# Two graph layers on one core: the lifting of the near-ones moved from ScalarE to TensorE, and DVE's additions set behind the next quotient

## The reference

```python
edge_index = jnp.stack([src, dst])
h = jnp.maximum(_layernorm(x), 0.0)
# layer 0: per edge and channel a softmax over the edges of one target
msg = h[src] + edge_attr;  s = msg * beta
e = exp(s - segment_max(s, dst)[dst]);  denom = segment_sum(e, dst)
agg = segment_sum(msg * e / denom[dst], dst)
x = x + (agg @ H + bias) + h            # H: 128x128, made of phm_rule and W
h = jnp.maximum(_layernorm(x), 0.0)
# layer 1: attention with 4 heads, 32 channels each
x = x + elu(segment_sum(alpha * (h @ W.T)[src], dst))
```

## Time and profile before

| | us |
|---|---|
| time, median of 3 runs | 2254.29 (2253.85 to 2254.93) |
| the profiled execution's own time | 2258.94 |
| its span in the profile | 2257.2 |
| layer 0's sweep, about | 60 to 1086 |
| last groups, then the batches | 1086 to 1133 |
| norm, `turn_h` and `layer_in` | 1133 to 1161 |
| layer 1 and the output | 1161 to 2257 |

### The profile page before, as it was taken

One profiled execution on the slowest core, in us unless ns is written; L12 is line 12 of the kernel. 1 busy time (PEld: TensorE's weight loads), 2 busy tenths in 40 slices (PEclk: granted clock), 3 DMA queues, 4 the chain that ended last, 5 costly groups with the idle time before them and its releaser, 6 DMA issues.

```text
span 2257.2 us, 61657 instructions
## 1 busy us (share of the span) xinstructions
PE 1940.5 (86%) x14541; PEld 1712.6 (76%) x14542; DVE 1986.2 (88%) x3873; ACT 1419.4 (63%) x3494; POOL 1644.8 (73%) x1739
## 2 busy tenths in 40 slices
PE   2888888888888888888879999999999899899997
PEld 1777777777777767777768888888888888888886
DVE  7999999999999999999759889888888888888886
ACT  3677777776777677777635555555555555555556
POOL 5777777777777777777527777777777777777775
PEclk9999999999999999999768989999999999999998
DMA  6444444444444444443023333333333333333331
GB/s 214 128 126 137 132 132 136 123 132 132 137 132 132 128 133 132 133 136 112 6 81 61 60 59 59 59 58 59 59 59 58 58 59 59 59 59 59 58 59 68
DMA packets 318697, 213.52 MB, mean 95 GB/s; under 512 B 169938, under 2 KB 279074, under 8 KB 318642
## 3 DMA queue, kind: packets, MB, share of 16 engines
q0 software_dynamic: 53184, 112.31, 20.8%
q1 hardware_dynamic: 264608, 100.15, 17.1%
q10 hardware_dynamic: 850, 0.43, 0.1%
HBM read 200.69 MB, written 10.29 MB: 93 GB/s over the span
## 4 chain that ended last, share of the span: by engine, by line
POOL 45%; issue 21%; DMA 13%; DVE 9%; PE 5%; ACT 5%; SPq 1%; ACTq 1%; POOLq 1%; DVEq 0%
POOL msg L683 25%; POOL ring_h L655 19%; DMA ring_h<-h_dram,meta_g 10%; DMA msg<-wx_dram,meta_g 3%; DVE seg_max L1117 2%; DVE sums L1112 2%; ACT banks L811 2%; PE sums L1383 1%; DVE onehot L1096 1%; PE sums L1440 1%; DVE prod L1281 1%; ACT acc L777 1%; SPq L556 1%; POOL wgt L703 0%; ACT sums L797 0%
## 5 line engine op out<-in xcount | busy, mean ns | idle before, releaser
L683 POOL DMA_INDIRECT msg<-wx_dram,meta_g x831 | 791.8, 953 | 304.4 <-issue 246.1
L655 POOL DMA_INDIRECT ring_h<-h_dram,meta_g x831 | 786.6, 947 | 265.7 <-issue 244.8
L1383 PE MATMUL sums<-onehot,prod 128*128 128x128 f32 x3296 | 686.4, 292 | 17.7 <-issue 5.9
L1383 PE MATMUL sums<-onehot,wgt 128*128 128x128 f32 x3296 | 668.9, 286 | 0.0
L1383 PEld LDWEIGHTS sums<-onehot,prod 128*128 128x128 f32 x3296 | 531.1, 203 | 52.0 <-issue 51.2
L1383 PEld LDWEIGHTS sums<-onehot,wgt 128*128 128x128 f32 x3296 | 532.5, 203 | 0.0
L777 ACT ACTIVATE acc<-sums 128x1022 f32 x410 | 419.9, 1024 | 0.1
L811 ACT ACTIVATE banks<-ring_h,sign 128x512 f32<-128x512 f32 x208 | 143.9, 692 | 266.8 <-DMA ring_h<-h_dram,meta_g 259.2
L1402 PEld LDWEIGHTS sums<-neg_ident,seg_max 128*128 128x128 f32 x1664 | 220.1, 193 | 100.5 <-issue 100.0
L1392 PE MATMUL banks<-ident,msg 128*128 128x128 f32 x832 | 137.4, 288 | 160.0 <-DVE msg L1135 159.9
L1112 DVE TENSOR_TENSOR_SCAN sums<-flags,seg_max,banks 4x512 f32<-4x512 bf16 x207 | 264.1, 1276 | 5.8 <-PE banks L1492 4.0
(11 more groups left out here) (215 smaller groups left out, 2887.4 us busy)
## 6 DMA issues: line engine op xcount, KB each, us to landing
msg<-in_edge_attr SPq DMA_DIRECT2D x207, 256.0 KB
flags<-flag_dram SPq DMA_DIRECT2D x52, 512.2 KB
window<-wx_dram SPq DMA_DIRECT2D x832, 2.0 KB
ring_h<-h_dram,meta_g POOLq DMA_INDIRECT x831
msg<-wx_dram,meta_g POOLq DMA_INDIRECT x831
wx_dram<-msg SPq DMA_DIRECT2D x13, 272.0 KB, 2.1
nodes<-in_x SPq DMA_DIRECT2D x6, 512.0 KB, 6.5
h_dram<-acc SPq DMA_DIRECT2D x12, 256.0 KB
```

The lines of the kernel that those rows point to most:

```text
L655: pool.indirect_dma_start(hg[0:n, s % HRING, b, :], None, h_dram, bass.IndirectOffsetOnAxis(ap=meta_g[0:n, s, b:b + 1], axis=0)).then_inc( ...
L683: pool.indirect_dma_start(msg[0:n, s, b, :], None, wx_dram, bass.IndirectOffsetOnAxis(ap=meta_g[0:n, s, b:b + 1], axis=0)).then_inc(L1["ga ...
L1383: ins = pe.matmul(where[:, j, bass.ds(off, P)], what[:, slot, b, :], onehot[:, s, b, :], start=(b == 0), stop=(b == GB - 1), skip_group_ch ...
```

## The change

The lift of a near-one is no longer a copy on ACT but a product with the identity on PE, in the same bank, with the same waits. Three of the thirteen lifts stand on PE between the last groups' work; the others stand ahead of `layer_out` of an earlier batch (`lift_near0(b + 2)` ahead of `layer_out(b)`). `layer_out(0)` now stands ahead of the last group's `sums0`. On DVE `quotient0` runs one batch ahead of `finish0`, not four. The near-ones have eight places, four of them in `ring_h`, whose use by layer 0's gathers is over once its last groups are lifted ([lifted0]); POOL's wait on [mid_lifted] begins at batch 8, not 4.

```diff
+        NEARS = 8
         def nears(b):
-            return (diff[:, b % 2, :], hn_row[:, b % 2, :])[b // 2 % 2]
+            if b % NEARS < 4:
+                return (diff[:, b % 2, :], hn_row[:, b % 2, :])[b // 2 % 2]
+            return ring_h[:, b % 4, :]
...
-                if b >= 4:
-                    pool.wait_ge(mid_lifted, b - 3)
+                if b >= NEARS:
+                    pool.wait_ge(mid_lifted, b - NEARS + 1)
+                elif b >= 4:
+                    pool.wait_ge(L0["lifted"], NG - HRING + b % 4 + 1)
...
-                act.activation(near_bank(b)[:, 0:w], nears(b)[:, 0:w], ACT.Copy).then_inc(mid_lifted, 1)
...
-            quotient0(1)
             dve.wait_ge(dve_sum, len(DVE_SUMS))
             dve.wait_ge(pool_sum, len(POOL_SUMS))
-            quotient0(2)
-            quotient0(3)
             for b in range(NBAT):
-                if b + 4 < NBAT:
-                    quotient0(b + 4)
+                if b + 1 < NBAT:
+                    quotient0(b + 1)
                 finish0(b)
...
+            def lift_near0(b):
+                w = LAST if b == NBAT - 1 else GE
+                pe.wait_ge(mid_near, b + 1)
+                if b < 2:
+                    pe.wait_ge(L0["scanned"], 2 * (NG - 1 + b))
+                else:
+                    pe.wait_ge(mid_agg, b - 1)
+                pe.matmul(near_bank(b)[:, 0:w], ident[:, :], nears(b)[:, 0:w], start=True, stop=True).then_inc(mid_lifted, 1)
...
             last(unturn0, 1)
+            lift_near0(0)
             pe.wait_ge(L0["onehots"], NG)
             pe.wait_ge(L0["added"], NG)
             last(sums0, 3, where=spare_sums0, free=1)
             last(unturn0, 0)
+            lift_near0(1)
             last(sums0, 2, free=1)
+            lift_near0(2)
             last(sums0, 1, where=spare_sums0, free=1)
-            last(sums0, 0, free=1)
...
-            straight(NBAT, [(0, layer_out)])
+            pe.wait_ge(L0["weighed"], NG)
+            pe.wait_ge(L0["multiplied"], NG)
+            layer_out(0)
+            last(sums0, 0, free=1)
+            for b in range(1, NBAT):
+                if b + 2 < NBAT:
+                    lift_near0(b + 2)
+                layer_out(b)
```

More of the change, by code:

```diff
@@ L849, in _ @@
             seed0(6)
-            lift_near0(0)
             last(merge0, 3, where=spare_sums0)
@@ L853, in _ @@
             last(weigh0, 0)
-            lift_near0(1)
             seed0(7)
@@ L857, in _ @@
             log0(8)
-            lift_near0(2)
             seed0(8)
@@ L861, in _ @@
             log0(9)
-            lift_near0(3)
             seed0(9)
@@ L865, in _ @@
             log0(10)
-            lift_near0(4)
             seed0(10)
@@ L869, in _ @@
             log0(12)
-            lift_near0(5)
             seed0(11)
             seed0(12)
-            for b in range(6, NBAT):
-                lift_near0(b)
             def turned1(b):
```

## The result

The changed kernel takes 2256.9 us in the median of 22 runs (2254.82 to 2261.33), the kernel before 2253.81 in 22 (2251.85 to 2256.03): a ratio of 1.0015, with a 95% interval of 1.001 to 1.0021. That is a loss of 3.1 us. It is smaller than the 0.2% that the prediction took as the least that can be told from no change, but with 22 runs of each the interval lies above 1. The forecast was 2257.5, 3.2 us more.

A forecast was written before the change was run, and what follows sets the result against it. ACT, then PE, was taken to bound the stretch between the sweeps; lifts +10.5, idle time -4.1 and clock -3.2 made +3.2 us, so 2262.1 profiled and, allowing for that execution's 4.65 above the median, 2257.5, range 2253.0 to 2261.5.

The forecast's parts named there:

- What bounds the stretch, and that a shift passes on: Between the sweeps: ACT bounds up to 1104.7, PE to 1131.5; a shift of layer 1's start passes one for one.
- The lifts, +10.5: On PE: twelve lifts at 0.86 us and one of 106 columns (0.18) cost 10.5 us, range 9.3 to 11.7.
- the rival of the cheap lifts: On PE: each lift costs only 0.22 us by the skill's page, giving 2249.7; chance 4%.
- The idle time, -4.1: On PE, from group 204's sums to batch 11's end: all 4.1 us of idle time are filled.
- a sum of 48.1: PE's new work from group 204's sums to batch 11's end, 48.1 us against 44.87 before.
- The clock, -3.2: On PE: with no hole the clock stays at 1.00, ten batches at 2.38 for 2.70, 3.2 us less.
- the 1.84 us hole: PE's idle time ahead of batch 2 in the kernel before, behind DVE's addition; the clock fell in the row behind it.
- The steady pace, 3.24, and one quotient ahead: PE needs 3.24 us per batch; DVE's ring has 0.9 us of slack, so one quotient ahead suffices.
- ACT's last merge: On ACT: comes no sooner than before, about 1102.3; only batches 11 and 12 need it, so it costs nothing.
- Clock into `layer_in`: Rival: the clock stays at 1.00 into layer_in, 3.0 us gained, 2254.5 in all; chance 15%.
- The clock falls among the batches: Rival: at clock 0.50 batches take 4.41 us in place of 3.24, 2269 from batch 1 on; chance 11%.
- A hole stays: Rival: the merge chain still holds the last sums, 2 us stay idle on PE, 2259.5 to 2261; chance 8%.

The follow-up runs named there:

- e1: The changed kernel with the thirteen lifts put back on ACT, the rest of the change kept: 2251.88 us, 0.9978 of the kernel before.
- e5: The changed kernel, lifts still on PE, but in the old order (layer_out(0) behind the last sums, four quotients ahead): 3354.35 us on a slow chip, 1.0016, undecided.
- e2: The changed kernel without any lift, DVE's quotient reading the near-one from SBUF: 2253.03 us, 0.9986 of the kernel before.
- f1: e1 with DVE writing the quotient so that PE reads it contiguously: 3343.91 us on a slow chip, 0.9975 of the kernel before, undecided.
- e3: The changed kernel with each lift's product issued twice in a row: 2269.76 us, 1.0062 of the kernel before.
- f2b: The changed kernel with DVE writing the quotient so that PE reads it contiguously, rerun on another chip: 2250.06 us, 0.9982 of the kernel before.
- h2: f2b with the stride on the quotient's inputs instead of its output, plus unneeded products in PE's norm waits: 2249.6 us, 0.9982 of the kernel before.
- h3: h2 with a third place for the quotient and DVE two quotients ahead: 2248.91 us, 0.9978 of the kernel before.
- e4: The changed kernel with three writes of unused buffers on DVE ahead of quotient 3, so PE must wait: 2266.92 us, 1.0045 of the kernel before.

## Why the prediction was right, and where its reasons were not

**What bounds the stretch, and that a shift passes on.** Right. Over nine kernels from -5.1 to +12.9 us, the shift of the last addition and the difference of the medians agree within 1.2 us.

**The lifts, +10.5.** Right in price and in that nothing hides them. Two records, 0.86 from start to start as the row had it, and a second copy of each adds 10.55. By the rival of the cheap lifts, 0.22 each, the time would have been 2249.7; the Trainium skill's 216 ns ("TensorE: Matmul & The Clock Gate", section "Back-to-back issue gap") doesn't hold for the f32 product of this kernel.

**The idle time, -4.1.** Right in size: PE is busy without a hole from 1084 to 1131 and beyond, and its work from the first lift to the last bias is 48.17 us (1084.44 to 1132.61), for a sum of 48.1. But the text puts it down to both parts of the change together (lifts gone from ACT, and more work on PE ahead of the last sums), and they aren't needed together. e1 fills it with the lifts still on ACT, and e5 fills it in the old order.

**The clock, -3.2.** Right in size, wrong in its reason, and so right by luck: "It fell in the row behind the 1.84 us hole; with no hole I keep it at 1.00". e1 has no hole, and the clock fell at 1103.1. What went with it is what PE was doing. In all four kernels whose batches had no lifts among them (before, e1, e2, f1) it fell, with holes or without, and in e5 it fell where they end; in the change, e3, f2b, h2 and h3 it stayed at 1.00 (0.99 in h2 and h3) to about the end of the lifts, though f2b has holes of 0.33 and 0.55. It shows in the mean granted clock of whole executions too, and not in the profiled ones alone: the middle values are 0.950 and 0.951 for before on two chips, 0.952 for e1 and 0.951 for e2, and 0.957 for the change and 0.958 for f2b. So -3.2 is not a gain of the closed hole, but a rebate on the lifts: they cost 10.5 and give back 3.2. Between e1 and the change the table has 7.5 us, where 10.5 - 3.2 is 7.3. Had I had to predict e1 by my reason, I would have been 3 us too low. A hole can take the clock as well, as e4 shows, where it fell 0.7 us into the hole and at the same place of the change it did not; whether the 1.84 us of before had a part in it stays open. Without them the clock fell all the same, in e1.

**The steady pace, 3.24, and one quotient ahead.** Right: 1099.32 to 1102.56, and no wait of PE for a quotient. ACT's last merge, forecast at about 1102.3, ends at 1100.37, which is 1102.5 with the 2.1, and nobody waits for it:

```profile
1099.34 1.03 ACT L783 ACTIVATE acc<-sums 128x1022 f32 x1
```

POOL's last near-one is done at 1106.8, and its last product at 1107.27, which with the 2.1 is 1109.4, two us later than the "about 1107" of the text; PE lifts the last at 1127.45, so it costs nothing.

**The rivals.** *Clock into `layer_in`*: it did not stay at 1.00, but in the profiled execution it was back at 1141.0, and the stretch from the addition to the gather is 2.1 us shorter than before's. The medians don't show those 2 us, since they give the 3.1 that the batches alone account for; so before's profiled execution was the unusual one in this. That fits its own time, 4.65 us above the median, and its mean granted clock of 0.948, but it is argued, not tested on before. *The clock falls among the batches*: its price is right, its "nothing in this stretch gave the clock back" doesn't carry over (e4), and so its 2269 was, by e4, too high. *A hole stays*: it didn't.

## What to carry to other kernels

A small operation that goes from another engine to the one that sets the pace costs its whole duration there, so take the price from the nearest row in the same type and test the parts of such a change apart: here the new order alone gains 5 us, and moving the lifts on top of it costs 8. When one stall has two cures, count its time once. And when a granted clock falls behind a hole, look for a stretch with the same work and no hole before you name the hole as the cause.

## What the runs showed of the hardware that I had not expected

- TensorE's granted clock fell from 1.00 to 0.50 (2.4 to 1.2 GHz) at 1103.1 in e1, behind 9.95 busy us of 10.00, and stayed at 0.50 with PE busy 22.40 of 22.40 us. It stayed at 1.00 with PE busy 25.36 of 29.40 (f2b, 1098.0 to 1127.4). It fell where the batches had no 512-column products among them, whether PE had gaps or none, and held where they did, but for the hole of e4.
- A stationary f32 operand read with a stride of four columns loads in 331 ns, a contiguous one in 192, and a batch of eight product records takes 2.13 us against 1.16 (the change and f2b). At 0.50 the strided batch loses only 0.11 (2.24, before), the contiguous one 0.92 (2.08, f1).
- DVE's quotient takes 1.05 us with an output written in steps of 128 elements (f2b) and 1.08 with both inputs read with a stride of four (h2), against 0.67 with neither.
- DVE with two f32 operands in SBUF and POOL's products wait for each other's end (e2): the quotient takes 1.06 to 1.51 us in place of 0.67, and POOL's longer product up to 1.60 in place of 1.27.
